# A four-layer network on one core: order of a state-space scan's matmuls and loads, and a minimum moved from VectorE to ScalarE and GpSimd

## The reference

```python
delta = softplus(dt_up @ (dt_down @ x) + dt_bias)      # step sizes, > 0
h_n[l] = exp(delta[l] * A_n) * h_n[l-1] + delta[l] * B_n[l] * x[l]
y[l] = sum_n C_n[l] * h_n[l] + D * x[l]
```

## Time and profile before

| | |
|---|---|
| median of 3 runs | 2953.14 us (2947.25 to 2956.69) |
| profiled execution | 2948.89 us, span 2947.0 us |
| stretch 2 to 110 us | earlier stages |
| stretch 110 to 328 us | step-size stage: VectorE busy 164.56, ScalarE 123.19, TensorE 122.73, GpSimd 88.10 |
| stretch 328 to 1985 us | scan: VectorE busy 1488.46, ScalarE 1269.56, GpSimd 1270.48, TensorE 1181.22 |
| stretch 1985 to 2946 us | later stages |
| granted TensorE clock, whole span | 0.908 of full |

### The profile page before, as it was taken

One profiled execution on the slowest core, in us unless ns is written; L12 is line 12 of the kernel. 1 busy time (PEld: TensorE's weight loads), 2 busy tenths in 40 slices (PEclk: granted clock), 3 DMA queues, 4 the chain that ended last, 5 costly groups with the idle time before them and its releaser, 6 DMA issues. The chain is left out here.

```text
span 2947.0 us, 81072 instructions
## 1 busy us (share of the span) xinstructions
PE 2192.8 (74%) x35284; PEld 1281.5 (43%) x35284; DVE 2387.3 (81%) x1941; ACT 1630.6 (55%) x2709; POOL 1553.1 (53%) x653
## 2 busy tenths in 40 slices
PE   6765366676677767777777777778985999799579
PEld 3442244444444444444444444434442555355444
DVE  5659689899898989899989889986787777699720
ACT  1646478778777777777777777863230000363220
POOL 0225578779686868788787868764000000198000
PEclk9976599999898999999999999998997999899689
DMA  1166654636546455546364554525005453100360
GB/s 48 82 197 267 211 142 131 168 108 165 142 119 157 119 148 136 136 126 167 106 168 123 138 130 132 153 77 191 0 1 142 114 129 98 43 8 8 82 88 24
DMA packets 149634, 348.19 MB, mean 118 GB/s; under 512 B 47611, under 2 KB 56704, under 8 KB 144288
## 3 DMA queue, kind: packets, MB, share of 16 engines
q1 hardware_dynamic: 148192, 338.88, 42.4%
q10 hardware_dynamic: 1088, 4.13, 0.6%
HBM read 245.73 MB, written 57.29 MB: 103 GB/s over the span
## 5 line engine op out<-in xcount | busy, mean ns | idle before, releaser
L843 POOL TENSOR_TENSOR l0c_hc<-l0c_cb,l0c_h 128x1536 f32<-128x1536 f32 x288 | 996.3, 3459 | 383.7 <-DVE l0c_h L814 374.3
L743 PE MATMUL ps<-l0c_img,l0c_vT 64*64 64x64 f32 x27648 | 576.4, 229 | 460.9 <-DVE l0c_r L796 393.5
L873 ACT ACTIVATE ps<-l0c_dlt,l0b_na 128x512 f32<-128x512 f32 (+1 forms) x1152 | 637.6, 577 | 370.1 <-DVE l0c_h L814 366.2
L743 PEld LDWEIGHTS ps<-l0c_img,l0c_vT 64*64 64x64 f32 x27648 | 501.8, 141 | 634.9 <-issue 590.1
L814 DVE TENSOR_TENSOR_SCAN l0c_h<-ps,l0c_last,l0c_r 128x768 f32<-128x768 f32 x384 | 696.7, 1814 | 2.9 <-ACT ps L873 1.9
L796 DVE SCALAR_TENSOR_TENSOR l0c_r<-l0c_r,ps 128x768 f32<-128x768 f32 x576 | 540.7, 939 | 149.7 <-PE ps L743 141.2
L882 ACT ACTIVATE l0c_r<-l0c_S,l0c_floor,l0b_na 128x768 f32<-128x768 f32 x576 | 585.6, 1017 | 0.0
L765 PE MATMUL ps<-l0c_hc,l0c_places 128*64 128x256 f32 (+1 forms) x2304 | 494.7, 553 | 6.8 <-POOL l0c_hc L843 3.4
L814 DVE TENSOR_TENSOR_SCAN l0c_h<-ps,l0c_r 128x768 f32<-128x768 f32 x192 | 336.2, 1751 | 0.7 <-issue 0.4
L1549 PE MATMUL ps<-l_prod,l_wa 128*96 128x384 f32 (+1 forms) x888 | 291.9, 492 | 25.5 <-DVE l_prod L1466 25.5
L830 POOL TENSOR_TENSOR l0c_img<-l0b_BC,l0c_places 128x768 f32<-128x768 f32 x192 | 283.3, 1478 | 7.7 <-DMA l0c_places<-in_places 7.7
(11 more groups left out here) (272 smaller groups left out, 2157.8 us busy)
## 6 DMA issues: line engine op xcount, KB each, us to landing
l0c_cb<-cf SPq DMA_DIRECT2D x768, 192.0 KB, 3.9
l0c_S<-S SPq DMA_DIRECT2D x72, 384.0 KB, 5.6
l0c_dlt<-dlt SPq DMA_DIRECT2D x72, 384.0 KB, 7.8
l_other<-l_p SPq DMA_DIRECT2D x22, 864.0 KB, 6.0
dlt<-l0s_dl SPq DMA_DIRECT2D x36, 384.0 KB, 2.3
v<-l0s_vv SPq DMA_DIRECT2D x36, 384.0 KB, 2.3
S<-l0s_So SPq DMA_DIRECT2D x36, 384.0 KB, 3.0
l0c_v<-v SPq DMA_DIRECT2D x36, 384.0 KB, 4.6
```

What stands on the lines that cost most here:

```text
L743: mm = pe.matmul(ps[64 * x:64 * x + 64, o:o + 64], vT[rows, u % 2, c, 64 * s:64 * s + 64], img[rows, q % NI, x, c, :], start=True, stop=True)
L843: pool.tensor_tensor(hc[:, p % NHP, :, :], rows, h[:, p % NH, :, :], ALU.mult).then_inc(s_hc, 1)
L873: act.activation(da[e % 2][:, part], dlt[:, u % 2, s, part], ACT.Exp, scale=na[:, 0, column(e)]).then_inc(done, 1)
```

## The change

In the step-size stage VectorE no longer takes minimum and addition (line 552). ScalarE takes the negative part of q with a Relu into `u` (`below`), and GpSimd subtracts it from `dl`; the running sum runs one unit later. Its unused operand is now the x place in PSUM instead of the logarithm's, so TensorE waits for it (`s_sum`). There are three buffers of `u` and five of `dl`, `vv`, `So` (ND). In the scan stage the loads of S and dlt are issued one at a time at g = 1, 2, 4, 5, and v at g = 0; TensorE issues `v_b` ahead of `turn`; `add_y` is cut into its two PSUM pieces (512 and 256 columns), one per step; turning moves to n = 3, 7, 11 and the earlier y goes behind the second piece. Nothing else changes.

```diff
 def l0_steps
-        NE, NW, ND = 3, 2, 4
+        NE, NW, ND = 3, 3, 5
 tensor, x_unit(i)
                     pe.wait_ge(s_s, i - 1)
+                    if i >= 5:
+                        pe.wait_ge(s_sum, i - 4)
 scalar
+            def below(i):
+                act.wait_ge(s_q, i + 1)
+                act.activation(u[:, i % NW, :], log(i), ACT.Relu, scale=-1.0).then_inc(s_rel, 1)
...
                     if i > NW:
-                        act.wait_ge(s_q, i - NW)
+                        act.wait_ge(s_dl, i - NW)
...
                     act.activation(e[:, i % NE, :], e[:, i % NE, :], ACT.Exp, scale=-1.0).then_inc(s_e, 1)
+                if i >= 2:
+                    below(i - 2)
...
                     if before(i - 1) is not None:
-                        act.wait_ge(s_dl, before(i - 1) + 1)
-                        if before(i - 1):
-                            act.wait_ge(s_sum, before(i - 1))
+                        act.wait_ge(s_rel, before(i - 1) + 1)
 vector
                     dve.scalar_tensor_tensor(ln, u[:, (i - 1) % NW, :], 1.0, ln, ALU.add, ALU.add).then_inc(s_q, 1)
-                    dve.wait_ge(s_q, i)
-                    if i >= 2:
-                        running_sum(i - 2, ln)
-                    dve.wait_ge(s_s, i)
-                    ds = dl[:, (i - 1) % ND, :]
-                    dve.scalar_tensor_tensor(ds, ln, 0.0, ds, ALU.min, ALU.add).then_inc(s_dl, 1)
-            running_sum(U - 1, log(U - 1))
+                if i >= 3:
+                    running_sum(i - 3, ps[:, base(i):base(i) + SEG])
+            running_sum(U - 2, ps[:, base(U):base(U) + SEG])
+            running_sum(U - 1, ps[:, base(U):base(U) + SEG])
 gpsimd, negative_u(i)
-                    pool.wait_ge(s_q, i - NW + 1)
+                    pool.wait_ge(s_dl, i - NW + 1)
...
+                pool.wait_ge(s_rel, i + 1)
+                pool.wait_ge(s_s, i + 1)
+                ds = dl[:, i % ND, :]
+                pool.tensor_tensor(ds, ds, u[:, i % NW, :], ALU.subtract).then_inc(s_dl, 1)
                 pool.wait_ge(s_dl, i + 1)
 def l0_scan
-        TURN, EMPTY, STORE = (4, 7, 10), (LAG + 4, LAG + 7, LAG + 10), LAG + 5
+        TURN, EMPTY, STORE = (3, 7, 11), (LAG + 4, LAG + 8, LAG + 11), LAG + 5
-        NLOAD = 4
+        LOADS = (1, 2, 4, 5)
 sync
-                if g == (0 if u == 0 else 1) and u + 1 < U:
-                    loads(u + 1)
+                if u + 1 < U:
+                    if g == 0:
+                        load_v(u + 1)
+                    if g in LOADS:
+                        load(u + 1, LOADS.index(g))
 tensor
-            for j in range(J + LATE):
+            for j in range(J + LATE + 1):
                 u, n = divmod(j, N)
+                if j + 1 < J:
+                    v_b(j + 1)
                 if n in TURN and u + 1 < U:
                     turn(u + 1, TURN.index(n))
-                if j + 1 < J:
-                    v_b(j + 1)
-                if j >= LATE and (j - LATE) % 2:
-                    add_y((j - LATE) // 2)
+                p, odd = divmod(j - LATE - 1, 2)
+                if p >= 0:
+                    add_y(p, odd)
+                    if odd:
+                        add_so_far(p)
 scalar, tanh(j)
-                    act.wait_ge(s_in[u % 2], (u // 2 + 1) * (16 * NLOAD))
+                    act.wait_ge(s_S[u % 2], 32 * (u // 2 + 1))
```

More of the change, by code:

```diff
@@ L331, in l0_steps @@
         s_x, s_ab, s_e, s_ln, s_u, s_up, s_q, s_s, s_dl, s_vv = map(sem, "x ab e ln u up q s dl vv".split())
-        s_out, s_one, s_sum, s_na = map(sem, "out one sum na".split())
+        s_out, s_one, s_sum, s_na, s_rel = map(sem, "out one sum na rel".split())
         s_dst = [sem(f"dst{i}") for i in range(ND)]
@@ L386, in _ @@
             for i in range(ND):
-                sp.wait_ge(s_dst[i], 16 * (U // ND))
-                sp.wait_ge(s_sst[i], 16 * (U // ND))
-                sp.wait_ge(s_vst[i], 16 * (U // ND))
+                sp.wait_ge(s_dst[i], 16 * len(range(i, U, ND)))
+                sp.wait_ge(s_sst[i], 16 * len(range(i, U, ND)))
+                sp.wait_ge(s_vst[i], 16 * len(range(i, U, ND)))
             sp.wait_ge(s_out, 16 * (1 + K * B))
@@ L506, in _ @@
                         evacuate(q)
+            below(U - 1)
             act.wait_ge(s_na, 2)
@@ L605, in l0_scan @@
         s_in = [sem(f"in{i}") for i in range(2)]
+        s_S = [sem(f"S{i}") for i in range(2)]
         s_v = sem("v")
@@ L692, in _, with load_v @@
         def _(sp):
-            def loads(u):
+            def load_v(u):
                 t, k, c0 = place(u)
-                i = u % 2
                 if u:
@@ L699, in loads, with load @@
                 sp.dma_start(v[:, :], d["v"][t * K + k, :, vc:vc + SEG]).then_inc(s_v, 16)
-                if u >= 2:
+            def load(u, part):
+                t, k, c0 = place(u)
+                x = part % 2
+                if u >= 2 and part == 0:
                     sp.wait_ge(s_scan, (u - 1) * N + 1)
[L702 to L705, removed]
+                tile, name = ((S, "S"), (dlt, "dlt"))[part // 2]
+                src = d[name][t * K + k].rearrange("(s p) c -> p s c", s=2)[:, :, c0:c0 + SEG]
+                sp.dma_start(tile[64 * x:64 * x + 64, u % 2, :, :], src).then_inc((s_S, s_in)[part // 2][u % 2], 16)
             sp.dma_start(places[:, :, :], a["places"]).then_inc(s_places, 16)
-            loads(0)
+            load_v(0)
+            for part in range(4):
+                load(0, part)
             sp.dma_start(Ds[:, :, :], a["Ds"]).then_inc(s_ds, 16)
@@ L719, in _ @@
                                      ).then_inc(s_cb[p % NG], 16)
-                if g == (0 if u == 0 else 1) and u + 1 < U:
-                    loads(u + 1)
+                if u + 1 < U:
[3 more added lines that the diff above has]
+                        load(u + 1, LOADS.index(g))
             for i in range(2):
-                sp.wait_ge(s_in[i], 16 * NLOAD * U // 2)
+                sp.wait_ge(s_S[i], 32 * (U // 2))
+                sp.wait_ge(s_in[i], 32 * (U // 2))
             sp.wait_ge(s_v, 16 * U)
@@ L756, in turn, with add_y, add_so_far @@
                 mm.then_inc(s_turn, 1)
-            def add_y(p):
+            def add_y(p, piece):
                 u, g = divmod(p, G)
[L760 to L767, removed]
+                if piece == 0:
+                    if g == 0 and u:
+                        pe.wait_ge(s_evac, u)
+                    pe.wait_ge(s_hc, p + 1)
+                lo, hi = pieces(PY)[piece]
+                for s in range(2):
+                    mm = pe.matmul(ps[64 * s:64 * s + 64, lo:hi], places[:, 0, :], hc[:, p % NHP, s, lo - PY:hi - PY],
+                                   start=(g == 0), stop=(g == G - 1))
+                if piece:
+                    mm.then_inc(s_y, 1)
+            def add_so_far(p):
+                u, g = divmod(p, G)
                 if place(u)[1] and 2 <= g < 2 + len(y_pieces(u)):
@@ L899, in _ @@
                 empty(0, part)
-            act.wait_ge(s_in[0], 16 * NLOAD)
+            act.wait_ge(s_in[0], 32)
             decay(0, own_part(0), s_own)
@@ L914, in _ @@
                         if (e + 1) % N == 0:
-                            act.wait_ge(s_in[(e + 1) // N % 2], ((e + 1) // N // 2 + 1) * (16 * NLOAD))
+                            act.wait_ge(s_in[(e + 1) // N % 2], 32 * ((e + 1) // N // 2 + 1))
                         decay(e + 1, own_part(e + 1), s_own)
```

## The result

| | median | ratio to before, 95% interval |
|---|---|---|
| before | 2952.27 us (2947.25 to 2956.69) | |
| changed kernel | 2872.73 us (2861.28 to 2874.5) | 0.9723, 0.9693 to 0.9753 |

That is 82 us less (2952.27 x 0.0277; interval 73 to 91). I had said 108 less and 2845 us; the range (2822 to 2900) holds the time, but the gain falls just short of the 85 to 132 us to which I had given 57%. The profiled execution took 2872.32 us, its span 2870.5.

A forecast was written before the change was run, and what follows sets the result against it. VectorE was taken to set the scan's pace, idling for late v*B from TensorE, and to bound most step-size units; -76 - 40 + 8 = -108 us gave 2845 us for the median, range 2822 to 2900.

The forecast's parts named there:

- Loads spread: Scan: TensorE's stalls are instruction blocks queued behind loads; spreading regains nearly all 87.8 us, 12 kept back, gain 76.
- rival 1: Scan: the stalls stay and only the order helps, -40 + 8, giving 2921 us; chance 16%.
- Half of the stalls left: Scan: case in which half of TensorE's stalls remain after spreading the loads, giving 2883 us; chance 12%.
- v_b first: Scan: v_b issued first and add_y halved remove TensorE's lateness; 63 - 23 = 40 us gained, bounds 20 and 54.
- The 12 us that I had left for other things: Scan, within the order's gain: 12 us kept back for the cold first unit and waits on ScalarE.
- Step sizes: Step-size stage: moving work from VectorE to ScalarE and GpSimd costs 8 us, bounds 0 and +15.
- loop (b): Step-size stage: loop by TensorE through the s_sum wait, 6.67 us and x_unit; 4.12 a unit at full clock, 4.80 at half.
- The pause: Step-size stage: VectorE's wait for unit 7's store behind the cf copies comes one unit of 4.4 us further on.
- The early part: Step-size stage, early units: cf copies go out some 7 us later, partly offset by five buffers; +2.6 us.
- Rival 2: Step-size stage: GpSimd's subtraction costs 3.64 us, pace 5.9 us, +35 in place of +3, giving 2877; chance 5%.
- Rival 3: Scan: spread loads keep the DMA queue filled, so most instruction blocks come late; slower, 3058 us at 1.5 us each; 6%.
- rival 4: Scan: VectorE's idle time moves to a C row, the decay or S; gain nil within 9 us, 2950; 4%.

The follow-up runs named there:

- e1: Kernel before with only the scan loads spread, TensorE's order and step sizes as before: 2881.35 us, ratio 0.974.
- e4: Kernel before with both scan edits (spread loads and TensorE's new order), old step sizes: 2851.87 us, ratio 0.9647.
- e2: Kernel before with only TensorE's new order, loads and step sizes as before: 2927.92 us, ratio 0.9902.
- e12: Changed kernel with VectorE's running sum issued ahead of q in the same pass: 2856.55 us, ratio 0.9673.
- e9: e4 with five buffers (ND = 5) in place of four, old step sizes otherwise: 2851.81 us, ratio 0.966.
- e10: e8 with GpSimd's negated u placed between subtraction and multiplication: 2887.48 us, ratio 0.9742.
- e5: e4 with S and dlt loaded for the first two units only, the others computing with old values: 2820.43 us, ratio 0.955.
- e7: e4 with S and dlt in eight loads of 192 KB: 2837.35 us, ratio 0.9613.
- e8: Changed kernel without TensorE's wait on s_sum, the running sum reading dl as its unused operand: 2890.63 us, ratio 0.9751.

## Why the prediction was right, and where not

**Loads spread, -76: right alone, wrong beside the new order.** e1 gives -77, and in it the stalls fall to 15.5 us, 11.4 of them at v_b: nearly all go, as forecast. In the changed kernel 36.2 us stay at v_b, where I had said under 15, and 47.6 in all: it is the new order that brings them back (15.5 in e1, 34.9 in e4). The 9 us of queue that "a block tolerates very roughly" were drawn from one stall, and took the order to be without effect on them. The cause itself, which was only argued, is now shown: the stalls end where blocks of instructions land, and leaving the loads out takes those of e4 from 34.9 to 12.1 us, smaller loads to 22.4. The rule of rival 1 is that instruction fetch is mostly hidden (the Trainium skill, "Runtime: NRT & Kernel Launch", Instruction fetch mechanics). In this trace 205 of 245 blocks did cost TensorE no wait, so "mostly" agrees; but the other 40 cost 62.3 us, and what rival 1 drew from the rule, that spreading the loads gives nothing, is wrong. Half of the stalls left was to give 2883; three quarters are left and the time is 2873; my reading, not tried by itself, is that a short stall often ends before VectorE needs v*B. VectorE's idle time in the scan is 66 us (1548.7 - 1482.4), where I had said 30 to 40.

**v_b first, -40: over-sized.** It measured -29 alone, and -27 beside spread loads (e4 less e1). The order itself does what the steps said: 0.57 to 0.7 us at n = 13 in most late units. The 12 us that I had left for other things were too few: in e2 the stalls grew from 62.3 to 97.3 us. This is the step that failed: I took order and stalls as two separate sums, "the number of matmuls is the same", though a new order puts other instructions behind the same loads. Which block each stall waited for can be read from the trace; why more of them come late with the new order is left open.

**Step sizes, +8: nearly right alone (+9.5), by terms that were not.** Steady pace 4.51 for 4.55, and loop (b) as named, shown by e12; some luck in it, since the clock granted there was 0.63 and not 0.72, with which my own sum gives 4.65; Relu 0.80 and subtraction 1.81 us as taken; tail +2.4 for +2.5. The pause went as worked out: one unit further on, 12.69 us. The early part was put at +2.6 and took 9.4; in it the B matmuls cost 1.0 us more in the first batch (11.73 for 10.73), 4.6 in the second and 0.6 in the third (7.10 for 6.49), by a clock that rose later. The 3 us left are near the 2.4 put for the Relu, but no run splits them. I had priced only engines' work there, and no bound for the clock.

**What the sum lacked.** -77 - 29 + 9.5 is -96, the three together -82. The 14 us between lie where the changed kernel's scan is 14.7 us longer than e4's with the same code, with 12.7 us more stalls. That the other step-size stage shifts where blocks end against the loads fits with this, but no run shows it. Chance of single executions may be a good part: the changed kernel's four runs span 13 us, and e9, with the old stage, and e10, with the new one, have the same 1538.4 us of scan. Rival 2 (GpSimd's subtraction at 3.64) would have given nearly this time, 2877, and is wrong: it took 1.81. Rival 3 and rival 4 didn't happen: VectorE's wait for v*B fell by 88 us and the scan by 90.

## What to carry to other kernels

An engine that waits for "issue" in the middle of a group of equal instructions, while the DMA engines are full, may be waiting for its own instructions: spread the loads, then make them smaller, before reordering the engine. Where two engines pass work around a ring, put first the operation that the slower part of the ring waits for: moving the running sum ahead of q gave 7 us of the stage for no work at all. And don't add up the gains of a reordering and of fewer stalls as if the stalls stayed where they were.

## What the runs showed of the hardware that I had not expected

- TensorE's waits without a releaser in the scan are waits for instructions: in eight profiles (before, the changed kernel, e1 to e5, e7) 259 of 264 end 1.25 to 1.71 us after a block of 16 KB on queue q8 has ended, the other five 1.11 to 1.24 us after.
- VectorE's running sum with two SBUF inputs and GpSimd's multiplication take turns: 1.81 and 1.82 us apart from each other, mostly 3.05 to 3.44 and 3.13 to 3.36 us when they meet (e8, e10). With one operand in PSUM, as in the kernels before and after, no running sum takes over 1.82 us and no multiplication over 1.86.
- The same 216 small matmuls take 7.10 or 11.74 us, by when the granted clock rises from 1.2 to 2.4 GHz; the time of the stage moves by about 7 us between kernels whose code there is the same (e4, e7).
- With S and dlt left out, TensorE still stalls 12.1 us in the scan, 2.4 of it in add_y.
